# The last step of an S4D convolution kernel, moved beside a top-32 attention in a one-core decoder kernel

## The reference, cut to what matters

```python
Q, K = (x_text @ Wq), (x_vision @ Wk)            # 4 heads of 32
topv, topi = jax.lax.top_k(scores, 32)           # the 32 best of 128 keys, for each query and head
probs = jax.nn.softmax(topv, axis=-1)
c_t = (attention over those keys, mean of the heads) @ V
scale_in, shift_in = split(c_t @ W_film_in + b_film_in)
x = layernorm(x_text) * (1 + mod_gate * scale_in) + mod_gate * shift_in
# s4d: the convolution kernel depends on weights alone
dtA = exp(log_dt)[:, None] * (A_re + 1j * A_im)              # 128 channels x 64 states
dC = C * (exp(dtA) - 1) / A
K = 2 * einsum('dn,dnl->dl', dC, exp(dtA[:, :, None] * arange(128))).real
y = causal convolution of x with K along the sequence + x * D_skip
```

## Time and profile before

| what | value |
|---|---|
| time of three runs, median (lowest to highest) | 3496.14 us (3494.99 to 3496.24) |
| the profiled execution, its own time | 3498.54 us |
| its span, first to last instruction | 3496.8 us |
| TensorE busy, mean granted clock | 2828.0 us (81%), 0.88 |
| VectorE busy | 1956.1 us (56%) |
| ScalarE busy | 1406.4 us (40%) |
| GpSimd busy | 1295.0 us (37%) |
| block 1 of the stage, from its first instruction to the next block's | 265.65 to 338.74 us |
| block 2, to the first Toeplitz load | 338.74 to 694.85 us |

### The profile page before, as it was taken

The page is one execution under the profiler, slowest core; times in us unless marked ns, Lnnn a source line. Parts: engine busy times, 40 slices in busy tenths (PEclk is TensorE's granted clock), DMA queues, the critical chain, the costliest instruction groups (busy, mean ns, idle before and its releaser), DMA issues. The chain is left out here.

```text
span 3496.8 us, 80020 instructions
## 1 busy us (share of the span) xinstructions
PE 2828.0 (81%) x32169; PEld 2018.1 (58%) x32169; DVE 1956.1 (56%) x5142; ACT 1406.4 (40%) x3183; POOL 1295.0 (37%) x1429
## 2 busy tenths in 40 slices
PE   6980466586767699799899986998789999979978
PEld 3550233274544477566699975665366666656657
DVE  5988988316455344466554444564855555536634
ACT  3540555416333555344322213552244334325544
POOL 3440333327121111344233333453833333325555
PEclk9995677558677899899899997998999999979989
DMA  3000000030000000000000000001000000000000
GB/s 97 3 2 2 1 1 1 11 95 1 1 6 17 15 2 1 38 3 3 8 1 1 1 1 16 2 2 40 4 2 2 2 2 2 2 8 2 3 0 24
DMA packets 24446, 37.21 MB, mean 11 GB/s; under 512 B 568, under 2 KB 21184, under 8 KB 23232
## 3 DMA queue, kind: packets, MB, share of 16 engines
q1 hardware_dynamic: 24096, 32.30, 2.9%
HBM read 30.07 MB, written 2.23 MB: 9 GB/s over the span
## 5 line engine op out<-in xcount | busy, mean ns | idle before, releaser
L1193 POOL TENSOR_TENSOR L_attn__qk<-L_attn__turned 128x512 f32<-128x512 f32 x128 | 161.4, 1272 | 352.8 <-DVE L_attn__turned L1302 352.8
L4218 PE MATMUL psum<-L_ffn__e_hT,weights 128*128 128x256 f32 x1024 | 244.8, 383 | 0.0
L777 DVE TENSOR_REDUCE L_xattn__nm<-psum 128x8 bf16<-128x1024 f32 x128 | 156.4, 1225 | 149.3 <-PE psum L970 143.0
L1302 DVE TENSOR_TENSOR L_attn__turned<-psum,weights 128x1024 f32<-128x1024 f32 x128 | 153.5, 1219 | 144.5 <-PE psum L1409 141.6
L4218 PEld LDWEIGHTS psum<-L_ffn__e_hT,weights 128*128 128x128 f32 x1024 | 186.8, 192 | 20.7
L4072 DVE TENSOR_TENSOR L_ffn__e_a<-L_ffn__e_sg,psum 128x512 f32<-128x512 f32 x128 | 88.1, 688 | 176.6 <-ACT L_ffn__e_sg L4064 176.5
L4064 ACT ACTIVATE L_ffn__e_sg<-psum 128x512 f32<-128x512 f32 x128 | 76.4, 597 | 258.9 <-PE psum L4218 258.9
L717 ACT ACTIVATE L_xattn__pT<-psum 128x1024 f32<-128x1024 f32 x128 | 124.0, 1021 | 59.0 <-PE psum L998 59.0
L4231 PEld LDWEIGHTS psum<-weights,L_ffn__e_a 128*128 128x128 f32 x1024 | 134.4, 191 | 7.3 <-DVE L_ffn__e_a L4072 0.7
L1409 PE MATMUL psum<-L_attn__xT,weights 128*128 128x256 f32 x512 | 136.2, 399 | 1.9 <-DVE L_attn__turned L1302 1.2
L4231 PE MATMUL psum<-weights,L_ffn__e_a 128*128 128x128 f32 x1024 | 135.0, 275 | 0.5 <-DVE L_ffn__e_a L4072 0.5
(11 more groups left out here) (676 smaller groups left out, 7744.6 us busy)
## 6 DMA issues: line engine op xcount, KB each, us to landing
L_xattn__toeplitz<-s4d_kernel SPq DMA_DIRECT2D x8, 1024.0 KB, 5.6
weights<-pack SPq DMA_DIRECT2D x1, 3328.0 KB, 10.2
weights<-pack SPq DMA_DIRECT2D x1, 3140.0 KB, 10.5
weights<-pack SPq DMA_DIRECT2D x1, 2370.0 KB, 9.3
out_dram<-X SPq DMA_DIRECT2D x1, 2048.0 KB, 8.7
weights<-pack SPq DMA_DIRECT2D x1, 1732.5 KB, 10.2
ctxT<-ctxT_in SPq DMA_DIRECT2D x1, 1536.0 KB, 22.1
weights<-pack SPq DMA_DIRECT2D x1, 1376.0 KB, 5.7
```

Of the source, the lines that this page charges most:

```text
L777: nc.vector.tensor_reduce(nm[:, n % 2, :].rearrange("p (g c) -> p g c", g=4)[:, 2 * u:2 * u + 2, 0:4], scores[u].rearrange("p g (i q) -> p ...
L1193: nc.gpsimd.tensor_tensor(qk[:, p % 2, u], turned[:, g % 2, :, 0:2 * P], turned[:, g % 2, :, 2 * P:4 * P], ALU.add).then_inc(qk_sb, 1)
L1302: nc.vector.tensor_tensor(turned[:, g % 2], proj[u % 2].unsqueeze(1).to_broadcast([P, 2, 4 * P]), k.w(name + "rope").rearrange("p (t q) -> ...
L4218: last = nc.tensor.matmul(bank[g % 2][:, 256 * c:256 * c + 256], k.w(name + w)[:, o:o + P], hT, start=True, stop=True)
```

## The change

- `pw` and `ws` no longer have tiles of their own: they lie in the weight buffer that the stage does not use. `kz` moves to the tiles that outlive block 1, and the four scratch tiles of `times` are halved.
- The loop of 8 turns leaves block 1. In block 2 GpSimd makes the two products and their difference, 16 positions x 64 states each: those of position 0 and 1 in its step 0, after `root(0)`, and those of position u+1 at the end of step u, after `modulated(u-1)`. Before each but the first it waits until VectorE has summed the one before.
- VectorE sums position u (`kernel_taps`) after round 2 of unit u, and adds `D_skip` after the last unit.
- The products lie in parts of `UY` and `FO` that the last units fill, so ScalarE waits in `filmed(7)` and `flipped(6)` until all eight sums are made.
- SyncE's store of `kz`, with its wait, moves to block 2; block 1's SyncE waits for its two mask loads.

```diff
--- before.py
+++ after.py
@@ -2458,6 +2458,12 @@
             text_gate = hold("text_gate", [P, NB])
             film_bias = hold("film_bias", [P, 4 * DM])
             film_rows = hold("film_rows", [3, 4 * DM], BF16)
+            kz = hold("kz", [P, 2 * P])
+            spare = k.weights[1 - BUFFER[stage]]
+            taken = (FINE + 1) * NN
+            pw = [spare[:, taken * i:taken * i + taken].rearrange("p (m n) -> p m n", n=NN) for i in range(2)]
+            ws = [spare[:, 2 * taken + COARSE * NN * i:2 * taken + COARSE * NN * (i + 1)].rearrange("p (m n) -> p m n", n=NN)
+                  for i in range(2)]
             with ExitStack() as ctx:
                 def sb(what, shape, dt=F32):
                     return ctx.enter_context(nc.sbuf_tensor(f"{name}_{what}", shape, dt))
@@ -2467,7 +2473,6 @@
                 over = [sb(f"over{i}", [3, 4 * DM]) for i in range(2)]
                 mask_text = sb("mask_text", [P, NB], U8)
                 text = sb("text", [P, NB])
-                kz = sb("kz", [P, 2 * P])
                 dt = sb("dt", [P, 1])
                 a_re, a_im = sb("a_re", [P, NN]), sb("a_im", [P, NN])
                 turn, whole, ang1, ang, nang, aang, cang = (
@@ -2477,14 +2482,12 @@
                 z1, nim = sb("z1", [P, NN]), sb("nim", [P, NN])
                 g_re, g_im = sb("g_re", [P, NN]), sb("g_im", [P, NN])
                 h_re, h_im = sb("h_re", [P, NN]), sb("h_im", [P, NN])
-                pw = [sb("pw_re", [P, FINE + 1, NN]), sb("pw_im", [P, FINE + 1, NN])]
-                ws = [sb("w_re", [P, COARSE, NN]), sb("w_im", [P, COARSE, NN])]
                 q2 = [sb("q2_re", [P, 1, NN]), sb("q2_im", [P, 1, NN])]
                 q4 = [sb("q4_re", [P, 1, NN]), sb("q4_im", [P, 1, NN])]
-                t4 = [sb(f"prod{i}", [P, FINE * NN]) for i in range(4)]
+                t4 = [sb(f"prod{i}", [P, FINE * NN // 2]) for i in range(4)]
                 step = sig.one("kernel_step", 1, 1)
                 masks_in = sig.one("masks_loaded", 32, 1)
-                dt_sb, angles, sines, kz_sb = (sig.one(n, 1, 1) for n in ("dt_sb", "angles", "sines", "kernel_sb"))
+                dt_sb, angles, sines = (sig.one(n, 1, 1) for n in ("dt_sb", "angles", "sines"))
                 magic = 12582912.0
                 two_pi_hi = 6.28125
                 two_pi_lo = float(2 * np.pi - two_pi_hi)
@@ -2496,9 +2499,7 @@
                     def _(sp):
                         sp.dma_start(mask_keys[:], k.masks[1][0].rearrange("(u j) g -> u (j g)", j=4)).then_inc(masks_in.sem, 16)
                         sp.dma_start(mask_text[:], k.masks[0]).then_inc(masks_in.sem, 16)
-                        sp.wait_ge(kz_sb.sem, kz_sb.base + 1)
-                        sp.dma_start(kernel_dram.ap(), kz[:]).then_inc(kernel_stored.sem, 16)
-                        sp.wait_ge(kernel_stored.sem, 16)
+                        sp.wait_ge(masks_in.sem, 32)
 
                     @block.scalar
                     def _(act):
@@ -2599,19 +2600,6 @@
                             times([a[:, m:2 * m, :] for a in ws], [a[:, 0:m, :] for a in ws],
                                   [a.to_broadcast([P, m, NN]) for a in f], [P, m, NN])
 
-                        p = [t[:].rearrange("p (m n) -> p m n", n=NN) for t in t4]
-                        for a in range(COARSE):
-                            for i in range(2):
-                                last = tt(p[i], pw[i][:, 0:FINE, :], ws[i][:, a:a + 1, :].to_broadcast([P, FINE, NN]),
-                                          ALU.mult)
-                            link(last)
-                            link(tt(p[2], p[0], p[1], ALU.subtract))
-                            o = P - 1 + FINE * a
-                            link(nc.vector.tensor_reduce(kz[:, o:o + FINE], p[2], AX.X, ALU.add))
-
-                        tt(kz[:, P - 1:P], kz[:, P - 1:P], w("D_skip"), ALU.add).then_inc(kz_sb.sem, 1)
-
-
             with ExitStack() as ctx:
                 def sb(what, shape, dt=F32):
                     return ctx.enter_context(nc.sbuf_tensor(f"{name}_front_{what}", shape, dt))
@@ -2645,11 +2633,32 @@
                 halves, moments, var_eps, rstd_sb, shift_sb, xh_sb = (
                     event(n) for n in ("halves", "moments", "var_eps", "rstd", "shift", "xhat"))
                 ones_set = event("ones_set")
+                kre_sb, kim_sb, kdiff_sb, kz_sb, kernel_sb = (
+                    event(n) for n in ("kre_sb", "kim_sb", "kdiff_sb", "kz_sb", "kernel_sb"))
+                pk = [UY[:, NB - 8:NB, :].rearrange("p j d -> p (j d)").rearrange("p (f n) -> p f n", n=NN),
+                      FO[:, NB - 4:NB, :].rearrange("p j d -> p (j d)").rearrange("p (f n) -> p f n", n=NN)]
 
                 with nc.Block() as block:
+
+                    @block.sync
+                    def _(sp):
+                        sp.wait_ge(kernel_sb, 1)
+                        sp.dma_start(kernel_dram.ap(), kz[:]).then_inc(kernel_stored.sem, 16)
+                        sp.wait_ge(kernel_stored.sem, 16)
 
                     @block.gpsimd
                     def _(pool):
+                        def kernel_products(a):
+                            if a >= 1:
+                                pool.wait_ge(kz_sb, a)
+                            for i, done in ((0, kre_sb), (1, kim_sb)):
+                                nc.gpsimd.tensor_tensor(pk[i], pw[i][:, 0:FINE, :],
+                                                        ws[i][:, a:a + 1, :].to_broadcast([P, FINE, NN]),
+                                                        ALU.mult).then_inc(done, 1)
+                            pool.wait_ge(kre_sb, a + 1)
+                            pool.wait_ge(kim_sb, a + 1)
+                            nc.gpsimd.tensor_tensor(pk[0], pk[0], pk[1], ALU.subtract).then_inc(kdiff_sb, 1)
+
                         nc.gpsimd.memset(ones_bf[:], 1.0).then_inc(ones_set, 1)
 
                         def root(u):
@@ -2698,6 +2707,10 @@
                             if u >= 1:
                                 chosen(u - 1)
                                 modulated(u - 1)
+                            if u == 0:
+                                kernel_products(0)
+                            if u + 1 < COARSE:
+                                kernel_products(u + 1)
 
                     @block.scalar
                     def _(act):
@@ -2757,6 +2770,8 @@
                             last.then_inc(xh_sb, 1)
 
                         def filmed(u):
+                            if u == UNITS - 1:
+                                act.wait_ge(kz_sb, COARSE)
                             act.wait_ge(v_ps, u + 1)
                             if u >= 1:
                                 act.wait_ge(c_ps, u)
@@ -2776,6 +2791,8 @@
                                                      ACT.Copy).then_inc(film_sb, 1)
 
                         def flipped(u):
+                            if u == UNITS - 2:
+                                act.wait_ge(kz_sb, COARSE)
                             act.wait_ge(flip_ps, u + 1)
                             nc.scalar.activation(UY[:, 4 * u:4 * u + 4, :].rearrange("p j d -> p (j d)"), KV[:],
                                                  ACT.Copy).then_inc(flip_sb, 1)
@@ -2866,6 +2883,11 @@
                             nc.vector.tensor_tensor(den[:, 2], den[:, 1],
                                                     text_gate[:, 4 * u:4 * u + 4].unsqueeze(2).to_broadcast([P, 4, heads]),
                                                     ALU.mult).then_inc(w_sb, 1)
+
+                        def kernel_taps(a):
+                            dve.wait_ge(kdiff_sb, a + 1)
+                            o = P - 1 + FINE * a
+                            nc.vector.tensor_reduce(kz[:, o:o + FINE], pk[0], AX.X, ALU.add).then_inc(kz_sb, 1)
 
                         for u in range(UNITS):
                             for r in range(rounds):
@@ -2883,8 +2905,13 @@
                                 replaced(u, r, 1)
                                 if r == 0 and u >= 1:
                                     inverse(u - 1)
+                                if r == 2:
+                                    kernel_taps(u)
                         inverse(UNITS - 1)
                         weights(UNITS - 1)
+                        dve.wait_ge(kz_sb, COARSE)
+                        nc.vector.tensor_tensor(kz[:, P - 1:P], kz[:, P - 1:P], k.w(name + "D_skip"),
+                                                ALU.add).then_inc(kernel_sb, 1)
 
                     @block.tensor
                     def _(pe):
```

## The result

The changed kernel takes 3456.81 us (median of four runs, 3451.43 to 3459.5) against 3495.56 for the kernel before in four runs; the ratio is 0.9888, with a 95% interval of 0.9871 to 0.9905. Forecast were 3456.1 us and 3447 to 3464. The profiled execution took 3459.5 us for a span of 3457.7.

A forecast was written before the change was run, and what follows sets the result against it. VectorE alone bounds block 1's loop; a chain from engine to engine paces the attention. -41.2 + 1.2 = -40.0 us brings the profiled 3498.54 to 3458.5, the median to 3456.1 us; range 3447 to 3464.

The forecast's parts named there:

- The loop and the store: End of block 1: removing the VectorE-only loop and the store with its wait saves 41.2 us, 1.7 the store.
- The first sum: Unit 0 of the attention, where VectorE is the path: position 0's sum adds 1.2 us.
- The other sums: Units 1 to 7, before reciprocals that wait for ScalarE: sums cost 0, or 8.5 us if the cover were gone.
- The products: GpSimd in the attention: three operations of 2.36 us, 7.2 us a position, cost 0; 43 us were the hole not there.
- the hole: GpSimd's 8.38 us idle between its last addition with root and diag; 7.2 us of work fits with 1.2 to spare.
- The cushion: Behind diag, the first ex waits another 1.91 us for ScalarE's exl, so diag may be that late in most units.
- ScalarE's and SyncE's waits: Attention: flipped(6) waits for the eighth sum, SyncE's store comes after the last weights; both claimed to cost 0.
- The lock: VectorE instructions with two SBUF inputs and GpSimd's SBUF reads exclude each other; costs nothing at the weights, by placement.
- Rival 2: Products overfill GpSimd's idle time, 3462 at 3.7 us each, or SBUF exclusion delays the weights, 3470; chance 0.06 for both.
- rival 3: Attention: VectorE's searches and GpSimd's products exclude each other, 67 us added against 41.2 saved, 3522; chance 0.02.
- Rival 1: Granted clock falls out differently over the attention's seven unit pitches, -8 to +6 us, 3448 to 3462; chance 0.18.
- my own marks for being wrong: Wrong if GpSimd operations exceed 3 us, diag stops waiting, pitch exceeds 40.3, or savings at first Toeplitz load and end differ over 3.

The follow-up runs named there:

- taps_first: Changed kernel with three more VectorE sums into an unused place behind the first sum, in unit 0; 3455.24 us in one run.
- taps_later: Changed kernel with three more VectorE sums into an unused place in each of units 1 to 7, 21 in all; 3458.34 us in one run.
- extra1: Changed kernel with one more GpSimd product into an unused place for each of positions 2 to 7, before root; 3457.32 us in one run.
- extra3: Changed kernel with three more GpSimd products into an unused place for each of positions 2 to 7, before root; 3482.77 us, eight runs.
- store_moved: Kernel before with only SyncE's store of kz and its wait moved to the start of the attention block; 3494.63 us in one run.
- powers_pool: film_slot with the 54 repeated-squaring operations moved from VectorE in block 1 to GpSimd at the attention's start; 3433.72 us, ratio 0.9831 to the kernel before.
- no_work: Changed kernel without GpSimd's 24 products, VectorE's 8 sums and ScalarE's waits for them; 3452.01 us, ratio 0.9882 to the kernel before.
- film_slot: Changed kernel with products before GpSimd's film wait, sums before waiting reciprocals, products in the unused weight buffer, no ScalarE waits; 3448.75 us, ratio 0.9878.

## Why the prediction was right

*The loop and the store.* -41.2 forecast, -41.19 measured, of it 1.7 and 1.72 for the store. The windows view said that nothing else ran in those 39.4 us, and this is why the term could be taken whole.

*The first sum.* +1.2 forecast; 1.1 by the first `diag` of eight kernels, with a scatter of 0.6, and taps_first, in which three more come out whole, shows that this place has no cover. The length of the block alone, +0.11 us, would have hidden it: C was 1.6 us shorter in the profile after.

*The other sums.* 0 forecast. VectorE's wait fell by 10.3 us and nothing moved; the three sums more a unit of taps_later still fit but for 0.1 us in all.

*The products.* 2.36 us each forecast, 2.35 measured (the mean of 24 is 2.344 to 2.352 by kind): the fixed part and the slope from three rows of other shapes held. 1.2 us of the hole were to be left, and 1.26 are. The cushion behind it, which I had read from one row, stands in extra1 and extra3: without it extra3 would have cost 34 us and not 24. The change itself does not use it.

*ScalarE's and SyncE's waits.* 0 forecast. The eighth sum ends at 595.74 and the `flipped` that needs it starts at 614.18, 18.4 us later; I had reckoned with some 10 of cover, in part because I put the sum behind the unit's last round and not behind its third.

*The lock.* I kept the weights free of it by their place in time, and the profile after agrees. Rival 2 had the right mechanism (extra3 shows 2.15 us instead of 0.16), only not in this kernel; rival 3, in which searches and products exclude each other, is refuted by `MATCH_REPLACE8`'s unchanged length and by A and B.

*The clock.* Rival 1 did happen, though small: C is 1.6 us shorter after than before, and its length follows the granted clock (last section). Two things in my account of it were wrong. I took 38.25 us as the shortest step and 40.22 as the longest; 36.57 occurs in the kernel after, and 41.36 in store_moved and powers_pool. And I leant on three runs that agreed within 1.25 us, where later runs of the kernel before spread further: eleven beside the first experiments reach from 3490.47 to 3496.78, nine beside the last from 3481.8 to 3501.49.

*A mark that was met.* One of my own marks for being wrong was met: the saving at the first Toeplitz load (694.85 - 652.61 = 42.24 us) and at the end (39.03) differ by 3.2, more than the 3 I had allowed. 2.96 of this lie in the rest of the kernel, which took between 2721.65 and 2734.02 us in ten profiles with the same instructions there. The mark was set too tight for such a spread.

*Luck.* The sum agreed with the median to 0.7 us, and in part by luck. Between the two profiled executions the stage started 1.16 us earlier, the attention gained 1.6 us in C, and the rest of the kernel took 2.96 longer; none of this was forecast, and the three together come to 0.2. The saving itself, by the medians measured together, is 38.75 us against 40.0. The terms of the sum are right to a few tenths, the measurement is not that fine.

## What to carry to other kernels

A stretch in which one engine works alone was worth its whole length here (39.47 us saved of 39.5), and the hole to move it into must be sized from the idle time that stands before the waiting instruction in the timeline, with the order of the streams in mind, not from an engine's busy share. Look at what the late instruction's first reader waits for anyway: that second wait is cover too, and it was worth up to 1.9 us a step here. Where a difference is a few us, compare the pieces of a trace that cannot depend on TensorE's clock, and keep VectorE's instructions with two SBUF inputs out of the time of long GpSimd ones.

## What the runs showed of the hardware that I had not expected

*The clock of one and the same piece differs from step to step and from profile to profile.* In the seven profiles whose steps have the same schedule (before, after, no_work, store_moved, taps_first, film_slot, powers_pool) A and B agree to 0.3 us, while C, whose instructions never differ, is 92.08 to 94.79; over all ten it reaches 98.21. ScalarE's timeline of the kernel after has the piece from the copy of `cT` to the first film copy in two steps:

```profile
359.93 0.60 ACT L2784 ACTIVATE L_xattn__front_cT<-psum 128x512 f32<-128x512 f32 x1 [1.27 <-PE psum L2981]
363.15 0.38 ACT L2789 ACTIVATE L_xattn__front_film<-psum 128x256 f32<-128x256 f32 x1 [2.62 <-PE psum L2992]
...
437.40 0.60 ACT L2784 ACTIVATE L_xattn__front_cT<-psum 128x512 f32<-128x512 f32 x1 [1.79 <-PE psum L2981]
441.77 0.38 ACT L2789 ACTIVATE L_xattn__front_film<-psum 128x256 f32<-128x256 f32 x1 [3.78 <-PE psum L2992]
```

It is 3.22 us in the one and 4.37 in the other. The windows view of these two stretches shows why:

```profile
core 0: us, PE busy (x) PEld busy (x) DVE busy (x) ACT busy (x) POOL busy (x), PEclk, DMA share, GB/s
359.90:363.20 3.30, 3.21 (x39) 1.48 (x37) 3.30 (x15) 0.65 (x2) 0.00 (x0) 1.00 0.00 0
437.40:441.80 4.40, 4.28 (x39) 1.83 (x37) 4.40 (x33) 0.62 (x2) 0.00 (x0) 0.76 0.00 0
```

39 matmuls in both, at a granted clock of 1.00 in the one, full speed (2.4 GHz), and 0.76 in the other, a mix of the two levels. The whole of C goes this way. In each of the first six steps it holds 55 or 56 recorded matmuls, and in all ten profiles its length goes with the granted clock: 11.8 us at 1.00, 13.4 to 13.5 at 0.83 to 0.87, 14.4 to 14.6 at 0.79 or 0.80. The longest of these is in the first step of extra1, in the windows view:

```profile
358.89:374.31 15.42, 12.34 (x56) 5.58 (x56) 15.42 (x98) 3.26 (x9) 0.00 (x0) 0.72 0.00 1
```

Length times clock, summed over the seven steps, is 77.6 to 78.7 us in every profile, so the clock accounts for nearly all of C's differences.

What sets the one clock or the other I have not tried, and one question stays open with it. The block is 356.22 us after, 359.57 in film_slot and 361.00 in taps_later, with C at 92.08, 94.67 and 97.64. The three kernels in which the steps hold more work than the changed kernel's, extra1, taps_later and extra3, have the three longest C of all, 95.82, 97.64 and 98.21. With one profile of each kernel this can be chance, or moved work can cost a few us through the clock, though no piece of the schedule shows it. For the change itself no such cost is seen: C is shorter after than before. That executions of one kernel differ is on record only for the whole of it: the kernel before took 3481.8 us at a mean granted clock of 0.884 and 3501.49 at 0.879.

*GpSimd's f32 product of two inputs follows one line over a range of 16 in size.* By the fixed part of 0.185 us and the slope of the prediction, two of them take 4.7 us at 1024 elements a partition, 1.46 at 256 and 0.64 at 64; powers_pool has 4.66, 1.35 to 1.41, and 0.54 to 0.60. At the small sizes the line is 0.02 to 0.05 us too high for each.
